# One decoder layer in a single launch: the order of helper work around its engines' queues is rewritten in four places

## The chip, the cores and the metric

The kernel runs on one core of one Trainium2 chip, in one launch. The metric is the device time of that launch in microseconds (us), the median over several runs. The core's engines are TensorE (PE: matmuls and transposes, with PEld for its weight loads), VectorE (DVE), ScalarE (ACT), GpSimd (POOL) and SyncE (SP, which here only issues DMAs). Each works through its own list of instructions in order and meets the others at semaphores.

## The reference, cut to what matters

Input x is (2, 1024, 256) float32: 2 batches, 1024 tokens, 256 features; the kernel cuts the 2048 tokens into 4 blocks of 512 and each block into 4 tiles of 128.

```
# 1 gated linear attention, 16 heads, DK = 8, DV = 16
q, k, v = x@Wq, x@Wk, x@Wv;  gk = log_sigmoid(x@Wgk1@Wgk2 + b)/16
h_t = h_{t-1}*exp(gk_t) + k_t v_t ;   o_t = (q_t * 8**-.5) h_t
x = layernorm(x + (rmsnorm(o)*gnw*silu(x@Wg)) @ Wo)
# 2 cross attention: each token attends to 64 of 64 context rows, given by an index
#   list with repeats; the kernel counts how often each row is named
x = layernorm(x + softmax(q k[idx]^T) v[idx] @ W_out)
# 3 causal self attention, 16 heads, then 8 experts, top 2, gelu
h = ln1(x); a = attention(h)@Wo + bo + x
h2 = ln2(a); w = softmax over the two best of (h2@Wr + br)
x = layernorm(sum_e w_e * (gelu(h2@w1_e + b1_e)@w2_e + b2_e) + a)
```

## The kernel before, in words

The program is four `nc.Block`s, one behind another. In each block every engine has its own list, written by hand.

**First block, `front` (0 to about 210 us).** The recurrence is a hardware scan along the 1024 tokens. There are NJ = 32 steps `jj` (2 batches by 16 value columns). In a step VectorE does three 128x1024 operations: `product(jj)` (L521, the k-v product out of PSUM), `state(jj)` (L526, the scan) and `output(jj)` (L531, times q). Its loop runs `state(jj)`, then `product(jj+1)`, then `output(jj)`. Other VectorE work is slipped into this loop at a named step, either behind `state(jj)` or behind `output(jj)`: `parts_lo(n)` (L514, low half of a split of the values, needed by PE and waiting for ScalarE's `parts_hi(n)`, L680), `x_lo` (L505, waits for ScalarE's `x_hi`, L650), `log_sigmoid(1)` (L511, waits for ScalarE's logarithm, L666), `out_means(m)` (L836, waits for ScalarE's `out_square(m)`, L832), and `out_gated(m)` (L845 to L849, waits for ScalarE's `out_root(m)`, L840). All `out_` helpers finish token block m; blocks 0 and 1 share one buffer, so `out_square(1)` comes behind `out_copy(0)` (L857), and that behind PE's transposes of what `out_gated(0)` wrote.

ScalarE has a list by the same `jj`. Into its gaps go 65 operations `signs` (L695, one 128x1024 comparison each, for counting the context indices). The list `taken` says how many of them are done by each step. In the steps with jj a multiple of 4, ScalarE copies the head sums (`sums_out`, L685), does one sign, then copies what PE has turned meanwhile (`tokens`, L688).

**Third block, `attend` (about 356 to 628 us).** Eight groups of four heads, `g` = 0 to 7. PE computes scores in units for the row maxima (VectorE, L2074), turns the maxima into rows (`turn`), computes scores again for the exponentials (ScalarE, L2012) and multiplies by values (`pv`, L1859). `warm(n, bank)` issues n matmuls of 128x512 whose result nobody reads (L1866). They stand at the start, ahead of `turn(0)` (7), behind the first unit of group 1 (3), behind the work of each of the first three steps `c` of group 0 (2 each), and at the end (2 and 2).

The last group is written out apart: its quads of exponentials (`last_exps(k)`, L2033; `quad_scores(k)` and `quad_sums(k)` on PE, k = 0 to 9) are interleaved with the routing work of token block 0. That work is one chain: `turn_sums`, `divide`, `turn_rows`, copies, `project` (L122), `residual` and statistics, `deviation` (ScalarE's square root, L2252), `normed` (L2308), `turn_normed` (L114), the two copies `rows_hi` and `normed_copy`, `logits` (L2237), the best two, and the weights. Scores of a quad reuse PSUM banks: bank b waits for the exponential of bank b-4. So `quad_scores(k)` waits for the first exponentials of quad k-1.

**Fourth block, `moe` (628.7 to 1384.6 us).** PE runs through s = 0 to 255 (32 pairs of expert and token block, 8 slices each): `first_layer` for s (6 matmuls, L2451), then `second_layer` for s-3 (6 matmuls, L2464). ScalarE applies gelu (L2533), VectorE splits the result (L2598, L2600). `first_layer(s)` waits for gelu(s-2). Weights come in quarters (n, q): SP loads a quarter to one of two raw buffers (L2193), ScalarE makes the high part (`weights_hi`, L2198), VectorE the low part (`weights_lo`, L2203). A load waits for the low part of the quarter two places earlier. `second_layer` of expert 0 waits for the low part of its quarter 3. The bias table is transposed by PE first (L2491) and copied by ScalarE (L2535).

Of the kernel before, what the change touches and what calls it, by code (L numbers as in the profile page):

```python
# [17 lines left out]
ACT = mybir.ActivationFunctionType  # L18
# [19 lines left out]
E = 8  # L38
# [23 lines left out]
class Kernel:  # L62
# [99 lines left out]
    def front(self, c):  # L162
# [58 lines left out]
        taken = list(itertools.accumulate((0, 1, 2, 3, 3, 5, 2, 1, 1, 1, 1, 2, 2, 3, 2, 3, 1, 2, 2, 2, 2, 2, 2, 2, 3, 3, 2, 2, 2, 2, 2, 1)))  # L221
# [3 lines left out]
        with nc.Block() as block:  # L225
# [268 lines left out]
            def _(e):  # L494
# [69 lines left out]
                for jj in range(NJ):  # L564
                    state(jj)
                    if jj == 2:
                        parts_lo(1)
                    elif jj == 6:
                        x_lo(3, 4)
                    elif jj == 11:  # L570
                        log_sigmoid(1)
                    elif jj == 12:
                        parts_lo(2)
                    elif jj == 18:
                        self.out_means(e, 0)
                    elif jj == 19:
                        parts_lo(3)
                    elif jj == 23:
# [6 lines left out]
                    if jj == 3:  # L585
                        x_lo(2, 4)
                    elif jj == 19:
                        self.out_gated(e, 0)
                        self.out_means(e, 1)
                    elif jj == 21:  # L590
# [42 lines left out]
            def _(e):  # L633
# [92 lines left out]
                for jj in range(NJ):  # L726
                    if jj % 4 == 0 and jj:
# [3 lines left out]

                        signs(range(taken[jj - 1], taken[jj - 1] + 1))
# [62 lines left out]
                    signs(range(taken[jj - 1] + (jj % 4 == 0) if jj else 0, taken[jj]))  # L795
# [758 lines left out]
    def attend(self, c):  # L1554
# [81 lines left out]
        with nc.Block() as block:  # L1636
# [93 lines left out]
            def _(e):  # L1730
# [172 lines left out]
                warm(7, 7)  # L1903
# [4 lines left out]
                warm(3, 7)  # L1908
                for g in range(NG - 1):
                    for c in range(NS):  # L1910
# [19 lines left out]

                        if g == 0 and c < PV_AT[0][0]:
                            warm(2, 7)
# [49 lines left out]
            def _(e):  # L1982
# [60 lines left out]
                last_exps(5)  # L2043
                last_exps(6)
                self.deviation(e, 0)
# [174 lines left out]
    def project(self, e, m, rb, ts=range(TB)):  # L2220
        if 0 in ts:
            e.wait_ge(self.VR.sem, self.VR.at("onT0", m))
            e.wait_ge(self.AR.sem, self.AR.at("onT1", m))
        last = self.token_major(e, self.onT, self.Wo, rb, ts)
        if TB - 1 in ts:
            last.then_inc(self.SR.sem, 1)
# [120 lines left out]
    def moe(self, c):  # L2347
# [54 lines left out]
        with nc.Block() as block:  # L2402
# [32 lines left out]
            def _(e):  # L2435
# [55 lines left out]
                e.transpose(PS[:, RB[0], 0:E * (NF + KD)], self.eb[:, :], self.ident[0:E * (NF + KD), 0:E * (NF + KD)]).then_inc(SM.sem, 1)  # L2491
# [31 lines left out]
            def _(e):  # L2523
# [11 lines left out]
                e.activation(bias[:, :], PS[:, RB[0], 0:E * (NF + KD)], ACT.Copy).then_inc(A.sem, 1)  # L2535
                e.wait_ge(A.sem, A.at("b1"))
                for s in range(NI * NF):
# [48 lines left out]
            def _(e):  # L2586
# [46 lines left out]
                def last_normed(k):  # L2633
# [6 lines left out]
                    last.then_inc(VL.sem, 1)  # L2640
                for s in range(NI * NF):
# [7 lines left out]
                    if s < 2:  # L2649
                        self.weights_lo(e, 0, 2 + s)  # L2650
                    elif 4 <= s < 8:
                        self.weights_lo(e, 1, s - 4)
# [97 lines left out]
```

## Time and the profile before

| | |
|---|---|
| median of 3 runs | 1386.23 us (1383.28 to 1386.34) |
| the profiled execution: its time | 1386.34 us |
| its span, first to last instruction | 1384.6 us |
| around the span | 1.74 us |
| mean granted TensorE clock | 0.982 |
| busy: PE / PEld / DVE / ACT / POOL | 93% / 69% / 71% / 47% / 10% |

Busy shares are averages over four blocks with different limits, so the profile is read block by block. The rows of a timeline give the start and the length of an instruction (or of several alike, then with xcount), and in brackets how long its engine had stood idle and who released it. An engine issues its next operation a little before the last one's recorded end, so the distance of two starts is used for pitch.

### The profile page before, as it was taken

Reading aid. Unit: us, or ns where it says so; the run is one execution under the profiler, and the core shown is the slowest. Engines: PE = TensorE matmul, PEld = TensorE weight load, DVE = VectorE, ACT = ScalarE, POOL = GpSimd, SP = SyncE. Lnnn points to the kernel's source line nnn. Section 1 sums busy time; section 2 is a strip of 40 time slices with the busy share of each in tenths; the row PEclk is TensorE's granted clock in tenths of the full one; section 3 lists DMA queues with packets and bytes.
Section 4 is the critical chain, followed back from the end, with each engine's and each line's share of the span. In section 5 each row is a group of like instructions: output and inputs, shape, how many; then the busy total and the mean of one; then the engine's idle time right before and its main releaser. Section 6 shows DMA issues by size and latency. Waiting matters only on the chain.

```text
span 1384.6 us, 18774 instructions
## 1 busy us (share of the span) xinstructions
PE 1291.7 (93%) x7481; PEld 953.4 (69%) x7481; DVE 977.6 (71%) x1409; ACT 647.3 (47%) x946; POOL 138.7 (10%) x217
## 2 busy tenths in 40 slices
PE   8786768999899999999999999999999999999997
PEld 6363437656655554556888888888888888888886
DVE  7998986798688888866666656655656555556566
ACT  5778564436457877784333333322322323232233
POOL 5000002000513434211000000000000000000000
PEclk9999989999999999999999999999999999999999
DMA  4000001001632221213000012110201102010001
GB/s 138 1 1 0 0 1 35 0 1 69 194 102 58 58 61 57 66 31 108 9 8 17 0 39 69 47 38 16 69 16 43 42 16 69 16 39 16 0 16 46
DMA packets 38599, 55.76 MB, mean 40 GB/s; under 512 B 8976, under 2 KB 23744, under 8 KB 38512
## 3 DMA queue, kind: packets, MB, share of 16 engines
q1 hardware_dynamic: 33328, 43.67, 10.3%
q0 software_dynamic: 3648, 10.09, 2.6%
q8 instruction: 59, 0.97, 0.3%
q10 hardware_dynamic: 1536, 0.81, 0.2%
q14 instruction: 28, 0.23, 0.1%
HBM read 43.73 MB, written 10.55 MB: 39 GB/s over the span
## 4 chain that ended last, share of the span: by engine, by line
PE 51%; DVE 2%; ACT 1%; issue 0%; ACTq 0%; DVEq 0%
PE PS L2451 24%; PE PS L2464 24%; PE PS L122 1%; PE PS L114 0%; PE PS L2477 0%; PE PS L2212 0%; PE PS L2237 0%; DVE OT_all L2607 0%; DVE r_st L2291 0%; DVE r_on L2308 0%; DVE r_on L2288 0%; PE PS L2489 0%; DVE X L2300 0%; DVE x_mid L2598 0%; ACT X L2570 0%
## 5 line engine op out<-in xcount | busy, mean ns | idle before, releaser
L2533 ACT ACTIVATE x_g<-PS,x_bias 128x512 f32<-128x512 f32 x256 | 175.9, 687 | 494.0 <-PE PS L2451 493.6
L2451 PE MATMUL PS<-x_h,x_w 128*128 128x512 f32 x1536 | 399.8, 396 | 0.6 <-ACT x_g L2533 0.6
L2464 PE MATMUL PS<-x_mid,x_w 128*128 128x512 f32 x1488 | 383.9, 393 | 1.2 <-DVE x_w L2203 1.2
L2451 PEld LDWEIGHTS PS<-x_h,x_w 128*128 128x128 f32 x1536 | 286.1, 188 | 66.1 <-ACT x_g L2533 1.5
L2464 PEld LDWEIGHTS PS<-x_mid,x_w 128*128 128x128 f32 x1488 | 279.4, 188 | 65.6 <-DVE x_w L2203 1.7
L2598 DVE CAST x_mid<-x_g 128x512 fp32r<-128x512 f32 x256 | 109.3, 427 | 271.6 <-ACT x_g L2533 271.5
L2074 DVE TENSOR_REDUCE a_M<-PS 128x2 f32<-128x1024 f32 (+1 forms) x144 | 170.6, 1222 | 24.9 <-PE PS L1782 19.3
L2600 DVE TENSOR_TENSOR x_mid<-x_g,x_mid 128x512 fp32r<-128x512 f32 x256 | 177.2, 692 | 8.8
L2012 ACT ACTIVATE f_parts<-PS 128x512 f32<-128x512 f32 x224 | 121.2, 600 | 34.4 <-PE PS L1836 27.9
L1859 PE MATMUL PS<-f_parts,aV 128*32 128x256 f32 (+1 forms) x960 | 74.2, 390 | 0.2 <-POOL f_parts L1673 0.2
L526 DVE TENSOR_TENSOR_SCAN qh<-decay,qh 128x1024 f32<-128x1024 f32 x32 | 73.0, 2283 | 0.0
L695 ACT ACTIVATE c_hot<-c_idxT,c_cid 128x1024 bf16<-128x1024 bf16 x65 | 70.7, 1137 | 3.5 <-PE PS L337 2.2
L2431 POOL DMA_DIRECT2D x_wb<-route_w x31 | 16.8, 541 | 476.3 <-DVE OT_all L2607 453.4
L1836 PE MATMUL PS<-aQ,aK 64*128 64x512 f32 x192 | 50.0, 489 | 0.0
L307 PE MATMUL PS<-vparts,g_sel 128*128 128x512 f32 x128 | 41.1, 448 | 8.6 <-DVE qh L521 7.6
L1836 PEld LDWEIGHTS PS<-aQ,aK 64*128 64x128 f32 x192 | 19.6, 183 | 39.7 <-ACT f_parts L2012 28.3
L2607 DVE SCALAR_TENSOR_TENSOR OT_all<-PS,x_bias,x_wb 128x512 f32<-128x512 f32 x62 | 46.2, 745 | 0.0
L1778 PE MATMUL PS<-aK,aQ 64*128 64x512 f32 (+3 forms) x256 | 36.0, 336 | 9.8 <-DVE a_M L2074 7.1
L1673 POOL TENSOR_SCALAR_AFFINE_SELECT f_parts<-f_parts 128x512 f32<-128x512 f32 x45 | 28.6, 635 | 164.6 <-ACT f_parts L2012 145.1
L2203 DVE TENSOR_TENSOR x_w<-x_raw,x_w 128x1024 fp32r<-128x1024 f32 x32 | 39.2, 1228 | 2.0 <-ACT x_w L2198 2.0
L521 DVE TENSOR_TENSOR qh<-PS,KT 128x1024 f32<-128x1024 f32 x32 | 38.6, 1207 | 2.7 <-PE PS L314 1.3
L531 DVE TENSOR_TENSOR qh<-qh,QT 128x1024 f32<-128x1024 f32 x32 | 38.9, 1216 | 0.0
(371 smaller groups left out, 1582.8 us busy)
## 6 DMA issues: line engine op xcount, KB each, us to landing
x_raw<-L_ffn_e_w SPq DMA_DIRECT2D x32, 512.0 KB, 3.7
qk_parts<-f_parts SPq DMA_DIRECT2D x16, 512.0 KB, 3.9
x_wb<-route_w POOLq DMA_DIRECT2D x31, 256.0 KB, 3.3
aK<-qk_parts SPq DMA_DIRECT2D x96, 64.0 KB, 2.6
aQ<-qk_parts SPq DMA_DIRECT2D x96, 64.0 KB, 2.5
X<-x SPq DMA_DIRECT2D x4, 512.0 KB, 7.5
out<-X SPq DMA_DIRECT2D x3, 512.0 KB, 2.9
O<-itok_BxSx SPq DMA_DIRECT2D x2, 256.0 KB, 7.8
```

Source lines behind the costliest of these rows:

```text
L526: e.tensor_tensor_scan(qh[:, jj % RQ, :], decay[:, batch(jj // HD)], qh[:, jj % RQ, :], 0.0, ALU.mult, ALU.add).then_inc(s_h, 1)
L695: e.activation(hot[:, n % RS, :], self.idxT[:, :], ACT.Sign, bias=self.cid[:, c:c + 1], scale=2.0).then_inc(s_sg, 1)
L1836: last = e.matmul(bank, K[q][R, s, tile(TB * h if kind == "k0" else kind)], Q[q][R, s, q0:q0 + BLK], start=True, stop=True)
L1859: last = e.matmul(PS[32 * j:32 * j + 32, 7, dst:dst + w], Vs[m % 2][:, kt, j, :], x, start=k in (0, 3) and half == 0, stop=k in (2, NQD - ...
L2012: e.activation(buf[k][:, j, :], PS[:, 4 + b % 3, :], ACT.Exp).then_inc(A.sem, 1)
L2074: e.tensor_reduce(dst, src, AX.X, ALU.max, negate=True).then_inc(VC.sem, 1)
L2451: last = e.matmul(PS[:, f % 2, :], w1[n % 2][u][:, kt, f * P:(f + 1) * P], self.rows(v, k)[:, kt, :], start=m == 0 and kt == 0, stop=m == ...
L2464: last = e.matmul(PS[:, 2 + 2 * (it % 2) + d, :], w2[n % 2][v][:, f, d * P:(d + 1) * P], mid[u][:, f % RM, :], start=f == 0 and m == 0, st ...
L2533: e.activation(g[s % RG][:, :], PS[:, f % 2, :], ACT.Gelu, bias=b1[:, n, f:f + 1]).then_inc(A.sem, 1)
L2598: e.tensor_copy(mid[0][:, f % RM, :], g[s % RG][:, :]).then_inc(V.sem, 1)
L2600: e.tensor_tensor(mid[1][:, f % RM, :], g[s % RG][:, :], mid[0][:, f % RM, :].bitcast(F32), ALU.subtract).then_inc(V.sem, 1)
L2607: e.scalar_tensor_tensor(out=(y if n else sumT[k])[:, d, :], in0=PS[:, 2 + 2 * (it % 2) + d, :], scalar=b2[:, n, d:d + 1], in1=wb[:, it % ...
```

## The change

1. **`front`, VectorE.** `parts_lo`, `x_lo(3)`, `log_sigmoid(1)` and `out_means(0)` move from behind `state(jj)` to behind `output(jj-1)`. `out_gated(0)` moves from behind `output(19)` to behind `output(18)`, and `out_gated(1)` from 21 to 20. `out_means(1)` stays behind `output(19)`.
2. **`front`, ScalarE.** The sign between `sums_out` and `tokens` goes, and the list `taken` is new. The total stays 65.
3. **`attend`.** 12 of the filling matmuls go: 3 of the 7 ahead of `turn(0)`, the 3 behind the first unit, 6 in group 0. In the last group `project` is one piece ahead of `quad_scores(5)`, scores come ahead of sums, `turn_normed` comes ahead of `quad_sums(6)` and `logits` ahead of `quad_sums(7)`; the two pairs of filling matmuls stand ahead of `project` and of `turn_normed` and no longer at the end. ScalarE's `deviation(0)` comes ahead of `last_exps(6)`.
4. **`moe`.** The bias transposes go to PSUM bank 0, and PE waits for ScalarE's copy of them before its first matmul. `weights_hi` and `weights_lo` of expert 0's quarters 2 and 3 run ahead of the loop (before: in s = 0 and 1). Expert 1's four quarters are made high in s = 1 to 4 and low in s = 2 to 5 (before: both in s = 4 to 7).

```
-taken = accumulate((0, 1, 2, 3, 3, 5, 2, 1, 1, 1, 1, 2, 2, 3, 2, 3, 1, 2, 2, 2, 2, 2, 2, 2, 3, 3, 2, 2, 2, 2, 2, 1))
+taken = accumulate((0, 1, 1, 2, 2, 3, 3, 2, 2, 2, 3, 2, 2, 3, 2, 3, *[2] * (HD - 1), 1))
 # front, VectorE
                     state(jj)
-                    if jj == 2: parts_lo(1)
-                    elif jj == 6: x_lo(3, 4)
-                    elif jj == 11: log_sigmoid(1)
-                    elif jj == 12: parts_lo(2)
-                    elif jj == 18: self.out_means(e, 0)
-                    elif jj == 19: parts_lo(3)
 ...
                     output(jj)
+                    if jj == 1: parts_lo(1)
-                    if jj == 3:
+                    elif jj == 3:
                         x_lo(2, 4)
+                    elif jj == 5: x_lo(3, 4)
+                    elif jj == 10: log_sigmoid(1)
+                    elif jj == 11: parts_lo(2)
+                    elif jj == 17: self.out_means(e, 0)
+                    elif jj == 18:
+                        parts_lo(3)
+                        self.out_gated(e, 0)
                     elif jj == 19:
-                        self.out_gated(e, 0)
                         self.out_means(e, 1)
-                    elif jj == 21:
+                    elif jj == 20:
                         self.out_gated(e, 1)
 # front, ScalarE
                         sums_out(jj // 4 - 1)
-                        signs(range(taken[jj - 1], taken[jj - 1] + 1))
                         tokens(jj // 4 - 1)
 ...
-                    signs(range(taken[jj - 1] + (jj % 4 == 0) if jj else 0, taken[jj]))
+                    signs(range(taken[jj - 1] if jj else 0, taken[jj]))
 # attend, PE
-                warm(7, 7)
+                warm(4, 7)
 ...
-                warm(3, 7)
 ...
-                        if g == 0 and c < PV_AT[0][0]:
-                            warm(2, 7)
 ...
                 quad_sums(NG - 1, 2)
-                self.project(e, 0, FREE, range(2))
-                quad_scores(5)
-                self.project(e, 0, FREE, range(2, TB))
-                for k in range(6, 8):
-                    quad_sums(NG - 1, k - 3)
+                warm(2, SPARE)
+                self.project(e, 0, FREE)
+                for k in range(5, 8):
                     quad_scores(k)
-                quad_sums(NG - 1, 5)
+                    quad_sums(NG - 1, k - 2)
+                warm(2, SPARE)
+                self.turn_normed(e, 0, FREE)
                 quad_sums(NG - 1, 6)
-                self.turn_normed(e, 0, FREE)
                 quad_scores(8)
+                self.logits(e, 0, FREE)
                 quad_sums(NG - 1, 7)
-                self.logits(e, 0, FREE)
                 quad_scores(9)
                 quad_sums(NG - 1, 8)
-                warm(2, SPARE)
                 quad_sums(NG - 1, 9)
-                warm(2, SPARE)
 # attend, ScalarE
                 last_exps(5)
+                self.deviation(e, 0)
                 last_exps(6)
-                self.deviation(e, 0)
 # moe, PE
-                e.transpose(PS[:, RB[0], 0:E * (NF + KD)], self.eb[:, :], ...).then_inc(SM.sem, 1)
+                e.transpose(PS[:, 0, 0:E * (NF + KD)], self.eb[:, :], ...).then_inc(SM.sem, 1)
+                e.wait_ge(A.sem, A.at("b1"))
 # moe, ScalarE (VectorE alike: weights_lo, with s in (2, 3, 4, 5) and s - 2)
+                for q in range(2, 4):
+                    self.weights_hi(e, 0, q)
 ...
-                    if s < 2:
-                        self.weights_hi(e, 0, 2 + s)
-                    elif 4 <= s < 8:
-                        self.weights_hi(e, 1, s - 4)
+                    if s in (1, 2, 3, 4):
+                        self.weights_hi(e, 1, s - 1)
```

## Rows read from the trace of the kernel before

**Rows 1.** Windows, first and last block: length; PE, PEld, DVE, ACT, POOL busy; clock.
```profile
0.00:210.00 210.00, 160.12 (x873) 101.85 (x874) 189.91 (x166) 142.14 (x152) 18.39 (x52) 0.91 0.08 23
...
628.70:1384.60 755.90, 743.49 (x3361) 607.58 (x3361) 452.81 (x812) 240.03 (x332) 18.86 (x35) 1.00 0.11 34
```

**Rows 2.** Timeline of VectorE, first block.
```profile
36.01 1.20 DVE L514 TENSOR_TENSOR vparts<-PS,vparts 128x1024 fp32r<-128x1024 f32 x1
...
44.49 1.23 DVE L505 TENSOR_TENSOR XTp<-PS,XTp 128x1024 fp32r<-128x1024 f32 x1 [0.57 <-ACT XTp L650]
...
57.64 1.22 DVE L505 TENSOR_TENSOR XTp<-PS,XTp 128x1024 fp32r<-128x1024 f32 x1 [0.83 <-ACT XTp L650]
...
65.49 2.28 DVE L526 TENSOR_TENSOR_SCAN qh<-decay,qh 128x1024 f32<-128x1024 f32 x1
...
81.04 1.20 DVE L511 SCALAR_TENSOR_TENSOR z<-z,decay 128x1024 f32<-128x1024 f32 x1
...
86.99 1.23 DVE L514 TENSOR_TENSOR vparts<-PS,vparts 128x1024 fp32r<-128x1024 f32 x1 [0.28 <-ACT vparts L680]
...
115.46 1.22 DVE L836 TENSOR_REDUCE go_ms<-z 128x64 f32<-128x1024 f32 x1 [0.53 <-ACT z L832]
...
131.71 1.22 DVE L836 TENSOR_REDUCE go_ms<-z 128x64 f32<-128x1024 f32 x1 [4.12 <-ACT z L832]
```

**Rows 3.** Timeline of ScalarE, first block.
```profile
34.68 1.03 ACT L680 ACTIVATE vparts<-PS 128x1024 fp32r<-128x1024 f32 x1 [3.70 <-PE PS L292]
...
79.79 1.06 ACT L666 ACTIVATE decay<-decay 128x1024 f32<-128x1024 f32 x1
...
85.93 1.02 ACT L680 ACTIVATE vparts<-PS 128x1024 fp32r<-128x1024 f32 x1 [2.10 <-PE PS L292]
...
114.36 1.06 ACT L832 ACTIVATE z<-O 128x1024 f32<-128x1024 f32 x1
```

**Rows 4.** Part 5 of the page, the sign operations.
```profile
L695 ACT ACTIVATE c_hot<-c_idxT,c_cid 128x1024 bf16<-128x1024 bf16 x65 | 70.7, 1137 | 3.5 <-PE PS L337 2.2
```

**Rows 5.** Windows of PE: length, busy (count), granted clock, DMA share, GB/s.
```profile
110.00:112.00 2.00, 0.00 (x0) 1.00 0.00 0
112.00:114.00 2.00, 1.86 (x17) 1.00 0.00 0
152.00:154.00 2.00, 0.00 (x0) 1.00 0.00 0
...
156.00:158.00 2.00, 2.00 (x10) 0.50 0.00 0
```

**Rows 6.** Timeline of PE, start of the third block.
```profile
398.29 0.73 PE L1866 MATMUL PS<-a_idr 128*128 128x512 f32 x2
```

**Rows 7.** Timeline of VectorE, start of the third block.
```profile
401.25 5.86 DVE L2074 TENSOR_REDUCE a_M<-PS 128x8 f32<-128x1024 f32 x5 [1.10 <-PE PS L1782]
```

**Rows 8.** Timeline of ScalarE, last group of the third block.
```profile
609.79 2.06 ACT L2033 ACTIVATE V<-PS 128x512 f32<-128x512 f32 x4 [0.63 <-PE PS L1836]
613.37 2.06 ACT L2033 ACTIVATE V<-PS 128x512 f32<-128x512 f32 x4 [1.52 <-PE PS L1836]
615.45 1.28 ACT L2252 ACT_TABLE_LOAD   x1
616.75 0.30 ACT L2252 ACTIVATE r_sd<-r_mv,eps 128x4 f32<-128x4 f32 x1
```

**Rows 9.** Timeline of PE, last group of the third block.
```profile
609.86 1.99 PE L122 MATMUL PS<-r_Wo,r_onT 128*128 128x256 f32 x8
...
618.73 1.09 PE L114 MATMUL PS<-ident,r_on 128*128 128x128 f32 x8 [0.88 <-DVE r_on L2308]
```

**Rows 10.** Timeline of PE, start of the fourth block.
```profile
637.49 1.66 PE L2464 MATMUL PS<-x_mid,x_w 128*128 128x512 f32 x6 [1.22 <-DVE x_w L2203]
```

**Rows 11.** Timeline of SP's queue, fourth block.
```profile
647.26 0.38 SPq L2193 DMA_DIRECT2D x_raw<-L_ffn_e_w  x1
```

**Rows 12.** Timeline of ScalarE, fourth block.
```profile
652.07 1.06 ACT L2198 ACTIVATE x_w<-x_raw 128x1024 fp32r<-128x1024 f32 x1 [0.74 <-DMA x_raw<-L_ffn_e_w]
```

More of the change, by code:

```diff
@@ L219, in front @@
         vt_banks = lambda n: 4 if n else 0
-        taken = list(itertools.accumulate((0, 1, 2, 3, 3, 5, 2, 1, 1, 1, 1, 2, 2, 3, 2, 3, 1, 2, 2, 2, 2, 2, 2, 2, 3, 3, 2, 2, 2, 2, 2, 1)))
+        taken = list(itertools.accumulate((0, 1, 1, 2, 2, 3, 3, 2, 2, 2, 3, 2, 2, 3, 2, 3, *[2] * (HD - 1), 1)))
         assert taken[-1] == NCTX
@@ L565, in _ @@
                     state(jj)
[L566 to L578, printed above, removed]
+                    if jj == 23:
                         self.out_rstd(e, 0)
@@ L584, in _ @@
                     output(jj)
-                    if jj == 3:
+                    if jj == 1:
+                        parts_lo(1)
+                    elif jj == 3:
                         x_lo(2, 4)
+                    elif jj == 5:
+                        x_lo(3, 4)
+                    elif jj == 10:
+                        log_sigmoid(1)
+                    elif jj == 11:
+                        parts_lo(2)
+                    elif jj == 17:
+                        self.out_means(e, 0)
+                    elif jj == 18:
+                        parts_lo(3)
+                        self.out_gated(e, 0)
                     elif jj == 19:
-                        self.out_gated(e, 0)
                         self.out_means(e, 1)
-                    elif jj == 21:
+                    elif jj == 20:
                         self.out_gated(e, 1)
@@ L2218, in turn_rows, with project @@
         self.transposes(e, self.on, 0, rb).then_inc(self.SR.sem, 1)
[L2220 to L2226, printed above, removed]
+    def project(self, e, m, rb):
+        e.wait_ge(self.VR.sem, self.VR.at("onT0", m))
+        e.wait_ge(self.AR.sem, self.AR.at("onT1", m))
+        self.token_major(e, self.onT, self.Wo, rb).then_inc(self.SR.sem, 1)
     def turn_normed(self, e, m, rb):
@@ L2490, in sums_turned @@
                     last.then_inc(SF.sem, 1)
-                e.transpose(PS[:, RB[0], 0:E * (NF + KD)], self.eb[:, :], self.ident[0:E * (NF + KD), 0:E * (NF + KD)]).then_inc(SM.sem, 1)
+                e.transpose(PS[:, 0, 0:E * (NF + KD)], self.eb[:, :], self.ident[0:E * (NF + KD), 0:E * (NF + KD)]).then_inc(SM.sem, 1)
+                e.wait_ge(A.sem, A.at("b1"))
                 for s in range(NI * NF):
@@ L2534, in _ @@
                 e.wait_ge(SM.sem, SM.at("b1"))
-                e.activation(bias[:, :], PS[:, RB[0], 0:E * (NF + KD)], ACT.Copy).then_inc(A.sem, 1)
+                e.activation(bias[:, :], PS[:, 0, 0:E * (NF + KD)], ACT.Copy).then_inc(A.sem, 1)
+                for q in range(2, 4):
+                    self.weights_hi(e, 0, q)
                 e.wait_ge(A.sem, A.at("b1"))
@@ L2640, in last_normed @@
                     last.then_inc(VL.sem, 1)
+                for q in range(2, 4):
+                    self.weights_lo(e, 0, q)
                 for s in range(NI * NF):
@@ L2648, in _ @@
                         summed(it - 1)
[L2649 to L2652, printed above, removed]
+                    if s in (2, 3, 4, 5):
+                        self.weights_lo(e, 1, s - 2)
                     if m + 1 < NB:
```

## Prediction, made before the change was run

> **What bounds the kernel now.** I read the windows by block first. In the last block TensorE is busy 743.5 of 755.9 us at full clock, in the first VectorE 189.9 of 210.0 us [rows 1]. The chain that ended last holds, for the last block, TensorE's two matmul lines nearly alone. So the kernel is four blocks in a row: the first goes by VectorE, the last by TensorE, and what a helper costs is read from the waits of these two. Then I read the timelines around each edit: VectorE and ScalarE in the first block, TensorE and ScalarE in the last head group, all of them where the experts start. The reader is to see in the bracket of a row who was late, and by how much. The rows that follow are used as terms.
>
> No edit changes an operation on data, except that 12 filling matmuls go. All else is order, so each term is a difference of waits.
>
> **First block, VectorE.** A helper moved from behind `state(jj)` to behind `output(jj-1)` comes one scan sooner: 2.28 us as recorded, 2.2 as pitch [rows 2]. It waits for its supplier on ScalarE that much longer, less what VectorE is already late, plus what the supplier is late.
> - `parts_lo(1)`: its supplier ends at 34.68 + 1.03 = 35.71 [rows 3]. The slot moves from 36.01 [rows 2] to 33.8. Wait 1.9, before 0. VectorE is 1.9 late, and 1.4 after `x_lo(2)`, whose wait of 0.57 [rows 2] is filled.
> - `x_lo(3)`: 0.83 before [rows 2]; 0.83 + 2.2 - 1.4 = 1.6, less about 0.5 since the sign ahead of `tokens` is gone and ScalarE gets there sooner: 1.1. VectorE is 1.6 late.
> - `log_sigmoid(1)`: the logarithm ends at 79.79 + 1.06 = 80.85 [rows 3], the slot moves from 81.04 to 78.8, that is 2.0 short. The new list asks for 4 signs in steps 7 and 8 where 2 stood. A sign is 1.14 [rows 4]; about half of the 2.3 goes into waits of ScalarE, so the supplier is 1.0 late. 2.0 - 1.6 + 1.0 = 1.4. VectorE is 3.0 late.
> - `parts_lo(2)`: steps 9 and 10 hold 5 signs where 2 stood, 3.4 more; ScalarE's wait of 2.10 ahead of this supplier [rows 3] takes 2.1 of them. Supplier late: 1.0 + 3.4 - 2.1 = 2.3. Wait 0.28 + 2.2 - 3.0 + 2.3 = 1.8, before 0.28 [rows 2]. VectorE is 4.5 late.
> - `out_means(0)`: from there to `out_square(0)` (114.36 [rows 3]) the lists hold 14 signs against 13, and in steps 12 and 16 the sign that used to run while TensorE turned the sums now runs after: 2.3 + 1.1 + 0.9 = 4.3 late. Wait 0.53 + 2.2 - 4.5 + 4.3 = 2.5, before 0.53 [rows 2].
> - `out_means(1)`: before, it stood right behind `out_gated(0)` and waited 4.12 [rows 2] for TensorE, a copy and the square. Now step 19 (scan and two products, 4.5) lies between: wait 0. `out_gated` itself waits 0.2 at most.
>
> New waits 1.9 + 1.1 + 1.4 + 1.8 + 2.5 = 8.7, old ones 0.57 + 0.83 + 0.28 + 0.53 + 4.12 = 6.3. **First block +2.4.** Bounds: suppliers on time after the first item, 1.9 - 6.3 = -4.4; suppliers one sign later each than reckoned, +5.
>
> **Third block, start.** VectorE waited 1.10 for the second unit of group 1 [rows 7]; two pairs of filling matmuls, 0.66 of pitch a pair, 0.73 as recorded [rows 6], stood ahead of that unit, but the exponentials that its neighbours wait for gain only some 0.3. The seven ahead of `turn(0)` only cover a wait for VectorE. Behind 401.25 VectorE runs five maxima without a gap [rows 7]. I take -0.5; bounds -1.1 (the whole wait) and +1.7 (clock, below).
>
> **Third block, last group.** Ahead of `quad_scores(5)` come the second half of the projection (1.99 recorded, 1.9 pitch [rows 9]) and a filling pair (0.66). So `last_exps(5)` starts at 609.79 [rows 8] + 2.5 = 612.3 and ends at 614.4. The projection's own end doesn't move: the pair replaces four score matmuls of the same length. Then ScalarE has the root: a table load of 1.28 [rows 8], the root, and a second load, some 2.9 together. They stood behind `last_exps(6)`; now they stand ahead, so `last_exps(6)` starts at 617.25, not 613.37 [rows 8]. Queued behind it on TensorE are `quad_scores(7)` (needs those banks), sums 5, a filling pair and only then `turn_normed`. Scores end at 617.25 + 2.06 + 0.2 = 619.5, sums 1.0, pair 0.66: `turn_normed` at 621.2, not 618.73 [rows 9], though its input is there by 617.3. The order behind is a chain of the same pieces (scores 8, exponentials, scores 9, POOL's mask, last sums, their copy on ScalarE), and the pair that stood at the very end was mostly under waits. **+2.6.** Bounds: -1.4, if only the earlier root counts, and +4.6 with a lower clock.
>
> The price of a switch of tables decides here. A load is recorded at 1.28, 615.45 to 616.73, and the root starts at 616.75 [rows 8]; I use that. The Trainium skill (ScalarE: Activation LUTs, "What ACT_TABLE_LOAD costs") adds a drain of 1.38 us to each load, 2.66 in all; by it the term would be 2.8 us more. By that rule the root could not start 0.02 us behind its load, as it does here.
>
> **Fourth block, start.** TensorE reached `second_layer(0)` 637.49 - 628.7 = 8.8 us into the block, the last 1.22 waiting for the low half of quarter 3 [rows 10]. Now both quarters are ready before the first gelu is split. The wait for the bias copy (an estimate: 0.45) and two high halves ahead of gelu(0) delay the third slice by 0.6, most of which its later neighbour takes up; `second_layer(0)` comes at 7.4, a gain of 1.4. Against it: ScalarE now stands at expert 1's quarters from s = 1 on and its gelus queue behind. A load takes 4.8 from issue (647.26 [rows 11]) to ScalarE's start (652.07, after waiting for the DMA [rows 12]). Quarter 3 of expert 1 is asked for at about 12.7 into the block, lands at 17.5, and gelu(5) comes at 19.0 to 19.7, where TensorE is ready at 18.8: 0.9 lost. **-0.5.** Bounds -1.4 and +1.5 (both late loads met in full).
>
> **The clock.** TensorE's granted clock stayed at 1.00 over an empty window at 110 to 112 us, but after another at 152 to 154 it stood at 0.50 (1.2 in place of 2.4 GHz) [rows 5]. Two new gaps are like these: about 615.4 to 617.6 and then four matmuls in two us; and the joint of the last two blocks, where the last filling pair is gone. I take one fall, in one of them. At half clock sums 5, the pair and `turn_normed` (2.7 us at full) take 2.7 more, or the first four slices twice their length with ScalarE covering half; about 1.5 reaches the end.
>
> **Sum**: 2.4 - 0.5 + 2.6 - 0.5 + 1.5 = +5.5. The profiled execution took 1386.34 us (span 1384.6 and 1.7 around it), 0.1 over the median. 1386.3 + 5.5 = 1391.8.
>
> **Rivals.**
> - *The clock holds.* All else as above: +4.0, 1390.3. For it: [rows 5], first two. Chance 0.22. It lies within 0.3% (4.2 us), which is what a measurement of this kernel can tell from no change.
> - *The first block gains* (not slower). ScalarE keeps up: with the sign ahead of `tokens` gone, everything that TensorE hangs on the sums comes a sign sooner, and the 4.12 counts. It decides at `parts_lo(2)`: if its supplier ends by 86.95, as now [rows 3], the later waits vanish. Block -4.4, the rest +1.6 without a fall: 1383.5. Against it: three more signs there than ScalarE has idle time for. Chance 0.22, with the tail's term also smaller in some of it, so that 0.08 is beyond 0.3%.
> - *Loads hold the gelus* (slower). If expert 1's loads land late, each blocked gelu stops TensorE: fourth block +1.5 in place of -0.5: 1393.8. For it: 4.8 of latency against 2.8 per slice. Chance 0.16.
> - *A load blocks longer than recorded* (slower). Would each of the two loads of the last group hold ScalarE for twice its 1.28, now that its exponentials queue behind them, the group would lose 2.6 more: 1394.4. The load in [rows 8] shows no such time: chance 0.03. The Trainium skill's page named above states a rule of this kind.
>
> The forecast itself has 0.37. **Chances**: slower by over 0.3% 0.37 + 0.16 + 0.03 = 0.56 less 0.02 for the forecast's own low end; within 0.3% 0.22 + 0.14 + 0.02; faster 0.08. **Range** 1384.5 to 1395.0: it leaves out the faster end of the second rival and the tail beyond the last; the forecast's own is 1389.5 to 1394.
>
> **What would show it.** Right: VectorE waits of 1 to 3 us at `parts_lo(1)`, `x_lo(3)`, `log_sigmoid(1)`, `parts_lo(2)` and `out_means(0)`, none at `out_means(1)`, the first block about 2.4 longer; ScalarE's root between exponentials 5 and 6, `turn_normed` about 2.5 later, the fourth block starting at 633 to 635; `second_layer(0)` 7.4 after its start. Wrong: signs that TensorE waits for less than I think, or a tail in which the scores of quad 7 don't wait for ScalarE.

## The result: 10.8 us slower, where 5.5 were forecast

| | before | after |
|---|---|---|
| median | 1385.38 us (1383.28 to 1386.34, 4 runs) | 1396.65 us (1394.47 to 1398.4, 4 runs) |
| ratio | | 1.0078, 95% interval 1.0058 to 1.0097: +8.0 to +13.4 us, +10.8 in the middle |
| profiled execution | 1386.34 us, span 1384.6, clock 0.982 | 1390.58 us, span 1388.9, clock 0.979 |

The profiled execution of the changed kernel is the fastest of its thirteen. The others ran 1391.5 to 1399.3 us, with a mean granted clock between 0.979 and 0.970. So its trace shows where the waits are, but only part of the loss: of 10.8 us it holds 4.3 in the span. The kernel before has one more run here than ahead of the prediction, which moved its median from 1386.23 to 1385.38.

Windows of the changed kernel, first and last block, columns as in [rows 1]:

```profile
0.00:210.00 210.00, 157.89 (x869) 100.81 (x870) 189.53 (x164) 141.63 (x152) 18.60 (x52) 0.91 0.08 23
...
632.84:1388.90 756.06, 744.80 (x3361) 608.50 (x3361) 452.61 (x812) 239.95 (x332) 18.82 (x35) 0.99 0.11 34
```

The last block keeps its length (756.1 for 755.9 us) and starts 4.1 us later. Timeline of VectorE in the first block, the operations of [rows 2] in the changed kernel:

```profile
35.89 1.22 DVE L514 TENSOR_TENSOR vparts<-PS,vparts 128x1024 fp32r<-128x1024 f32 x1 [1.85 <-ACT vparts L680]
...
56.72 1.23 DVE L505 TENSOR_TENSOR XTp<-PS,XTp 128x1024 fp32r<-128x1024 f32 x1 [0.68 <-ACT XTp L650]
...
80.20 1.23 DVE L511 SCALAR_TENSOR_TENSOR z<-z,decay 128x1024 f32<-128x1024 f32 x1
...
87.36 1.22 DVE L514 TENSOR_TENSOR vparts<-PS,vparts 128x1024 fp32r<-128x1024 f32 x1 [1.48 <-ACT vparts L680]
...
117.42 1.22 DVE L834 TENSOR_REDUCE go_ms<-z 128x64 f32<-128x1024 f32 x1 [2.15 <-ACT z L830]
...
131.66 1.21 DVE L834 TENSOR_REDUCE go_ms<-z 128x64 f32<-128x1024 f32 x1
...
139.29 0.55 DVE L843 RECIPROCAL go_rs<-go_rs 128x64 f32<-128x64 f32 x1 [1.97 <-ACT go_rs L838]
```

Four waits are where and as long as reckoned: 1.85 (1.9 forecast), 1.48 (1.8), 2.15 (2.5) and none where 4.12 stood. `x_lo(3)` waits 0.68 (1.1). `log_sigmoid(1)` doesn't wait (1.4 forecast), and `out_gated(1)` waits 1.97 (0.2). The block ends only 0.9 later than in the trace of before (first copy into `aug` at 212.4 against 211.6), but how little such a pair of traces says is shown below.

Timeline of ScalarE and then of TensorE in the last head group, against [rows 8, 9]:

```profile
611.93 2.06 ACT L2024 ACTIVATE V<-PS 128x512 f32<-128x512 f32 x4 [2.81 <-PE PS L1834]
614.01 1.28 ACT L2240 ACT_TABLE_LOAD   x1
615.31 0.30 ACT L2240 ACTIVATE r_sd<-r_mv,eps 128x4 f32<-128x4 f32 x1
615.62 1.28 ACT L2024 ACT_TABLE_LOAD   x1
616.92 2.07 ACT L2024 ACTIVATE V<-PS 128x512 f32<-128x512 f32 x4
```

```profile
617.57 1.96 PE L1834 MATMUL PS<-aQ,aK 64*128 64x512 f32 x4 [2.02 <-ACT V L2024]
...
621.99 1.67 PE L114 MATMUL PS<-ident,r_on 128*128 128x128 f32 x8
```

`last_exps(6)` starts at 616.92 (617.25 forecast). The scores of quad 7 wait 2.02 for it, and `turn_normed`, its input ready at 617.3, is queued behind them until 621.99 (621.2 forecast). The lengths show more: eight transposes take 1.67 where they took 1.09 [rows 9]. Windows of TensorE (length, busy, granted clock, DMA share, GB/s) show why, and two more such places:

```profile
394.00:396.00 2.00, 1.04 (x4) 0.65 0.00 0
402.00:404.00 2.00, 2.00 (x19) 0.50 0.00 0
...
618.00:620.00 2.00, 2.00 (x16) 0.97 0.00 0
620.00:622.00 2.00, 2.00 (x15) 0.50 0.00 0
622.00:624.00 2.00, 2.00 (x17) 0.68 0.00 0
634.00:636.00 2.00, 2.00 (x6) 0.50 0.00 0
```

The clock is at half (1.2 GHz) from some 395 to 405 us, where the fillers were removed, from 620 to 623, behind the 2 us without work, and from 633.5 to 637, just behind the joint to the fourth block. I had counted one fall. Between 364 us and the last ten us this execution has three, and that of before none; it lacks the other's fall at the joint of the second and third block, 356 to 363.

### The profile page after: what moved, and what is told of

The parts are those of the page before. It is cut to its first block, busy times and chain, and to the rows that moved or that the text cites. A ratio compares the mean times of both kernels' runs of the same rounds, so it can differ in the third digit from the quotient of the medians.

```text
span 1388.9 us, 18750 instructions
## 1 busy us (share of the span) xinstructions
PE 1291.1 (93%) x7469; PEld 954.1 (69%) x7469; DVE 978.2 (70%) x1409; ACT 646.8 (47%) x946; POOL 138.9 (10%) x217
## 4 chain that ended last, share of the span: by engine, by line
PE 50%; DVE 3%; ACT 1%; issue 0%; DMA 0%; ACTq 0%; DVEq 0%
PE PS L2439 24%; PE PS L2452 23%; PE PS L122 1%; PE PS L114 0%; PE PS L2465 0%; DMA x_raw<-L_ffn_e_w 0%; PE PS L2225 0%; DVE OT_all L2596 0%; DVE r_st L2279 0%; DVE r_on L2296 0%; DVE x_mid L2589 0%; DVE x_mid L2587 0%; DVE r_on L2276 0%; PE PS L2477 0%; PE PS L2203 0%
## 5 line engine op out<-in xcount | busy, mean ns | idle before, releaser
L307 PEld LDWEIGHTS PS<-vparts,g_sel 128*128 128x128 f32 x128 | 23.6, 202 | 25.0 <-DVE qh L521 15.6
```

The source lines that it names most:

```text
L307: last = e.matmul(PS[:, 2 * (jj % 2) + half, :], self.sel[:, j, :], vparts[:, u, n % 2, half * BLK:(half + 1) * BLK], start=u == 0, stop=u ...
```

## The experiments

Each ran in alternation with the kernel before. "+us" is the ratio less one, times the median of before (1384.7 to 1386.5). "Clock" is the mean over all executions; that of before was 0.9816 to 0.9823.

| kernel | +us (95% interval) | clock |
|---|---|---|
| the whole change | +10.8 (8.0 to 13.4) | 0.9741 |
| front_alone | +3.9 (2.2 to 5.5) | 0.9799 |
| warms_alone | +0.7 (-1.4 to 2.8) | 0.9791 |
| tail_alone | +7.1 (4.3 to 9.7) | 0.9783 |
| experts_alone | +1.5 (-0.3 to 3.3) | 0.9802 |
| tail_dev_back | +2.6 (0.8 to 4.3) | 0.9813 |
| dev_alone | +5.0 (3.3 to 6.7) | 0.9805 |
| tail_fill_back | +3.6 (1.7 to 5.5) | 0.9798 |
| dve_alone | +1.8 (0.0 to 3.5) | 0.9807 |
| signs_alone | +4.2 (2.4 to 6.0) | 0.9794 |
| signs_counts | +2.1 (0.7 to 3.5) | 0.9793 |
| signs_place | +1.0 (-0.3 to 2.2) | 0.9805 |
| experts_fill | +0.6 (-1.4 to 2.5) | 0.9811 |
| after_fill_back | +6.8 (4.4 to 9.2) | 0.9777 |
| after_fill_dev_back | +4.2 (2.2 to 6.1) | 0.9790 |
| after_three_back | -0.8 (-2.8 to 1.2) | 0.9814 |
| after_dev_signs_back | +1.8 (-1.0 to 4.6) | 0.9782 |
| joint_fill | -0.6 (-1.9 to 0.7) | 0.9814 |
| three_joint | -0.8 (-3.3 to 1.5) | 0.9823 |

### The four parts, each alone

The change's diff cut in four by place: first block (`taken`, the signs, VectorE's helpers), the fillers at the start of the third block, its last head group, the start of the fourth block. In the expectations theory Q lays a loss to waits in the engines' queues, theory C to TensorE's clock.

> Of the change only the first block's part: VectorE's helpers and the sign operations in their new places, the rest as before. Theory Q (the loss of each part is the wait that its queue gets): the waits seen in the trace of the changed kernel sum to some 7 us on VectorE against 6.3 before, the block ended 0.85 us later: +0.5 to +1.5 us, granted clock as before (0.982). Theory C (the loss is TensorE's clock, which falls more often): this part removes no TensorE work, so it is the one part in which C expects little too, 0 to +2 us; but if its time moves together with a lower mean granted clock, C has its hand here as well. The forecast had +2.4 us for it, and a rival -4.

> Of the change only the filler matmuls at the joint of the second and third block: 4 for 7 ahead of the turn, none behind the first units and none between the first scores. Theory Q: the path there is VectorE's and ScalarE's, and fewer matmuls in front of the scores give 0 to -1 us. Theory C: the fillers held the clock; without them TensorE runs at 1.2 GHz from some 394 to 405 us, in every execution, and the kernel is 1.5 to 4 us slower, with a mean granted clock lower by 0.004 or more.

> Of the change only the last head group: the projection in one piece, scores ahead of sums, the deviation ahead of the exponentials of group 6, the closing fillers moved forward. Theory Q: the root between two loads of ScalarE's tables stands ahead of an exponential that scores(7) waits for: +2.5 to +4 us by the end of the block and no more, at the clock of before. Theory C: the same +2.5 to +4 us, and on top of it the clock that falls at the end of the group and over the joint to the fourth block, where the fillers no longer stand: +4 to +7 us, with a lower mean clock than before in most executions.

> Of the change only the start of the fourth block: bias through bank 0, the first layer waiting for it, the copies of the weights' halves earlier. Theory Q: the second layer starts 0.3 us earlier after the block's start, the copies that wait for their loads cost nothing on TensorE: 0 to -0.5 us. Theory C: TensorE waits idle at the block's start for the bias, and its clock falls there: +0.5 to +2 us with a lower mean clock.

They sum to +13.2, within what 10.8 (8.0 to 13.4) allows: the loss is in the parts and not in their company. The last group is the largest, +7.1 where 2.6 stood, and the first block came out above its expectation. In the trace of tail_alone the stretch from `turn_rows` to `turn_normed` is 17.73 us (600.47 to 618.20) against 13.78 before (from 604.95 to the 618.73 of [rows 9]), and the fourth block's first matmul to `second_layer(0)` 9.54 against 8.78. Windows of TensorE in tail_alone:

```profile
612.00:614.00 2.00, 0.87 (x2) 0.74 0.00 0
616.00:618.00 2.00, 2.00 (x14) 0.50 0.00 0
630.00:632.00 2.00, 2.00 (x7) 0.51 0.00 0
```

warms_alone kept its promise about the clock and not about the time. Windows of TensorE:

```profile
392.00:394.00 2.00, 1.61 (x10) 0.50 0.03 8
396.00:398.00 2.00, 2.00 (x20) 0.50 0.00 0
400.00:402.00 2.00, 2.00 (x18) 0.50 0.00 0
```

All three traced kernels without these fillers have a clock of 0.80 over 385 to 410 us; all others, 17 traces, have 1.00. But its median is +0.7 and not +1.5 or more: what the clock costs there is about paid back by matmuls that no longer stand ahead of the units.

### The last group taken apart

tail_dev_back and dev_alone differ from tail_alone and from before in this alone:

```diff
                 last_exps(5)
-                self.deviation(e, 0)
                 last_exps(6)
+                self.deviation(e, 0)
```
(dev_alone: the reverse). tail_fill_back:
```diff
-                warm(2, SPARE)
                 self.project(e, 0, FREE)
...
-                warm(2, SPARE)
                 self.turn_normed(e, 0, FREE)
...
                 quad_sums(NG - 1, 8)
+                warm(2, SPARE)
                 quad_sums(NG - 1, 9)
+                warm(2, SPARE)
```

> The last head group's new order as in tail_alone (which measured +7.1 us), but ScalarE's deviation back behind the exponentials of group 6. Theory A (the deviation ahead of them is the loss: its two table loads and its root, 2.9 us, stand between scores(6) and the exponentials that free scores(7)'s banks, and turn_normed is queued behind scores(7)): exps(6) then follows exps(5) directly, the root comes about 0.7 us later after the first turn than in the kernel before, turn_normed 14.4 to 14.6 us after it (before 13.8, tail_alone 17.7); the kernel is +0.5 to +2.5 us against before. Theory B (the order on TensorE and the fillers' place are the loss, whatever ScalarE does): +5 us or more stay.

> The kernel before with one thing changed: the deviation ahead of the exponentials of group 6. ScalarE is idle there for 1.5 us before them, so of 2.9 us some 1.4 come to lie on them. Theory A: exps(6) 1.4 us later, scores(7) and sums(6) with it, turn_normed waits for sums(6) on the queue: +0.5 to +2 us. Theory B: what the deviation costs the exponentials it gives back to the chain of the routing, 0 +/- 0.7 us.

> As tail_alone, but the two pairs of filling matmuls stand behind the last sums as in the kernel before, not ahead of the projection and of turn_normed. Theory A: ahead of the projection they held exps(5) 0.6 us back, at the end they are hidden: +5.5 to +7 us stay of +7.1. Theory C (the clock at the joint): without them at the end TensorE falls to 1.2 GHz at the fourth block's start (tail_alone, 630 to 633 us), and with them there the clock holds at that place: the second layer starts within 8.9 us of the block's start, and +3.5 to +5.5 us stay.

Theory A holds. With the deviation back, 4.5 of 7.1 us are gone (the +2.6 that stay are at the top of its +0.5 to +2.5), and `turn_normed` comes 14.34 us behind `turn_rows` (607.26 to 621.60). Timeline of ScalarE in tail_dev_back: the exponentials of quads 5 and 6 run as one stretch of eight, and the root follows.

```profile
614.28 4.03 ACT L2030 ACTIVATE V<-PS 128x512 f32<-128x512 f32 x8 [2.81 <-PE PS L1836]
618.32 1.28 ACT L2246 ACT_TABLE_LOAD   x1
619.62 0.30 ACT L2246 ACTIVATE r_sd<-r_mv,eps 128x4 f32<-128x4 f32 x1
```

dev_alone was to cost 0.5 to 2 and cost 5.0: one line moved by one place. I had overlooked a wait. Timelines of ScalarE and of TensorE in dev_alone:

```profile
610.78 1.28 ACT L2252 ACT_TABLE_LOAD   x1
614.08 0.30 ACT L2252 ACTIVATE r_sd<-r_mv,eps 128x4 f32<-128x4 f32 x1 [2.02 <-DVE r_mv L2298]
614.40 1.28 ACT L2033 ACT_TABLE_LOAD   x1
615.69 2.06 ACT L2033 ACTIVATE V<-PS 128x512 f32<-128x512 f32 x4
```

```profile
616.34 2.26 PE L1836 MATMUL PS<-aQ,aK 64*128 64x512 f32 x4 [2.92 <-ACT V L2033]
...
622.11 1.75 PE L114 MATMUL PS<-ident,r_on 128*128 128x128 f32 x8
```

The root's table is loaded, and then ScalarE stands 2.02 us for VectorE's statistics, with exponentials queued behind whose scores ended at 612.4. TensorE stands 2.92 us, and its clock goes to half: 0.50 from 618 to 622 us. In the changed kernel `last_exps(5)` comes 7.0 us behind `turn_rows` and not 4.8 as here, so the root doesn't wait and TensorE's gap is 2.02; the rest is the same.

tail_fill_back stays at +3.6: 3.5 us less than tail_alone, though the intervals overlap. Its fourth block starts at full clock (1.00 over 628 to 638 us, tail_alone 0.83) and reaches `second_layer(0)` in 8.79 us, as before. Both statements of theory C came in, the time at the low edge of its +3.5 to +5.5; that of A didn't. But the trace doesn't show that the fillers held the clock. A fall stands just ahead of them, and over the whole end of the block the clock is what it is in tail_alone. Window of TensorE in tail_fill_back, then 580 to 640 us in tail_alone, tail_fill_back, dev_alone and tail_dev_back:

```profile
624.00:627.00 3.00, 3.00 (x28) 0.50 0.02 5
580.00:640.00 60.00, 53.09 (x422) 0.89 0.10 30
580.00:640.00 60.00, 54.26 (x424) 0.89 0.10 31
580.00:640.00 60.00, 54.02 (x449) 0.91 0.07 21
580.00:640.00 60.00, 54.66 (x489) 0.97 0.06 19
```

What the time at half clock follows here is the deviation. The five traces with it ahead of the exponentials of quad 6 (the first three of these kernels, the changed kernel and after_fill_back) have 7 to 14 us at half clock between 580 and 640 us, 11.6 in the mean. The fifteen others have 0 to 7, 2.9 in the mean, wherever the fillers stand. What the 3.5 us between tail_alone and tail_fill_back are stays open; that run moves both pairs and doesn't part them.

### The first block taken apart

dve_alone has only the moved helpers, signs_alone only what ScalarE's sign operations change, and that again in two:
```diff
-        taken = list(itertools.accumulate((0, 1, 2, 3, 3, 5, 2, 1, 1, 1, 1, 2, 2, 3, 2, 3, 1, 2, 2, 2, 2, 2, 2, 2, 3, 3, 2, 2, 2, 2, 2, 1)))
+        taken = list(itertools.accumulate((0, 1, 1, 2, 2, 3, 3, 2, 2, 2, 3, 2, 2, 3, 2, 3, *[2] * (HD - 1), 1)))
```
in signs_counts, and in signs_place
```diff
                         sums_out(jj // 4 - 1)
-                        signs(range(taken[jj - 1], taken[jj - 1] + 1))
                         tokens(jj // 4 - 1)
...
-                    signs(range(taken[jj - 1] + (jj % 4 == 0) if jj else 0, taken[jj]))
+                    signs(range(taken[jj - 1] if jj else 0, taken[jj]))
```

> Of the first block's part (which measured +3.9 us) only the places of VectorE's helpers; ScalarE's sign operations as before. Theory Q (a helper that comes an iteration before its input is ready stalls VectorE, and the chain of states behind it): all of the part's loss is here, +2.5 to +5 us. Theory S (the signs' new counts shift ScalarE, which then gives vparts, z and states later): 0 to +1.5 us here, and the rest with the signs.

> Of the first block's part only the sign operations' new counts on ScalarE (the part measured +3.9 us, VectorE's helpers alone +1.8 us). If the two add up: +1 to +3 us. If the signs cost nothing and the helpers only collide with them: 0 +/- 0.7 us.

> Of the signs' change (+4.2 us) only the new counts per step; one sign still stands ahead of tokens in every fourth step. If the counts are the cause (three or four signs in a row ahead of copies that TensorE waits for): +3 to +5 us. If the place is: 0 to +1 us.

> Only the sign ahead of tokens taken away, its work put behind the step's other copies, the counts as before. ScalarE then waits idle for TensorE's sums and turns in eight steps and does the sign after, when TensorE waits for copies: 1.1 us each, partly hidden. If this is the cause: +3 to +5 us, with ScalarE's waits ahead of L688 up by about 1 us each. If the counts are: 0 to +1 us.

It was mainly the signs: +4.2 (2.4 to 6.0) alone, above what was expected even if the two added up, against +1.8 (0.0 to 3.5) for the helpers. These two intervals overlap; the traces below and after_three_back point the same way. Timeline of VectorE in signs_alone, where every helper is in its old place, and in dve_alone:

```profile
81.05 1.22 DVE L511 SCALAR_TENSOR_TENSOR z<-z,decay 128x1024 f32<-128x1024 f32 x1 [1.56 <-ACT decay L666]
88.19 1.23 DVE L514 TENSOR_TENSOR vparts<-PS,vparts 128x1024 fp32r<-128x1024 f32 x1 [1.45 <-ACT vparts L680]
118.29 1.22 DVE L834 TENSOR_REDUCE go_ms<-z 128x64 f32<-128x1024 f32 x1 [2.17 <-ACT z L830]
134.46 1.22 DVE L834 TENSOR_REDUCE go_ms<-z 128x64 f32<-128x1024 f32 x1 [4.12 <-ACT z L830]
```

```profile
35.80 1.23 DVE L514 TENSOR_TENSOR vparts<-PS,vparts 128x1024 fp32r<-128x1024 f32 x1 [1.85 <-ACT vparts L680]
58.87 1.22 DVE L505 TENSOR_TENSOR XTp<-PS,XTp 128x1024 fp32r<-128x1024 f32 x1 [2.94 <-ACT XTp L650]
88.26 1.23 DVE L514 TENSOR_TENSOR vparts<-PS,vparts 128x1024 fp32r<-128x1024 f32 x1 [0.34 <-ACT vparts L680]
116.71 1.22 DVE L836 TENSOR_REDUCE go_ms<-z 128x64 f32<-128x1024 f32 x1 [0.55 <-ACT z L832]
137.79 0.55 DVE L845 RECIPROCAL go_rs<-go_rs 128x64 f32<-128x64 f32 x1 [0.70 <-ACT go_rs L840]
```

Three waits are new in the first, against 0, 0.28 and 0.53 in [rows 2]: together 4.4 us. The 4.12 stays. ScalarE's timeline of signs_alone shows a run of two and one of three signs, 2.17 and 3.22 us, ahead of the supplier of `parts_lo(2)`, which it reaches at 87.14 without the wait of 2.10 that it had [rows 3]. In dve_alone the helpers wait 1.85 and 2.94 for their early places, and the 4.12 is gone: about even. Counts and place make +2.1 and +1.0. Neither comes to the +3 to +5 of a single cause; the counts are told from nothing, the place isn't, and the two aren't told from each other.

The traces allow a second reading. The first block ends (first copy into `aug`) at:

| helpers, signs | traces | mean | lowest and highest |
|---|---|---|---|
| old, old | 9 | 211.4 us | 208.9, 214.3 |
| new, old | 4 | 210.0 | 209.2, 210.9 |
| old, new | 1 | 213.3 | |
| new, new | 4 | 214.5 | 212.4, 215.5 |

(signs_counts ends at 211.9, signs_place at 213.8.) So by the means the part is +3.1, the signs +4.5 with the new helpers around them, the helpers nothing or a small gain. But nine traces of one and the same first block differ by 5.4 us: the 0.9 us that the first pair of traces showed can't be told from chance.

The clock goes with these ends. Up to the copy, six of the nine old ones have 34 to 38 us at half clock and end at 208.9 to 211.6; the other three have 44 and end at 213.4 to 214.3. Of the new, new ones the changed kernel has 38 and ends at 212.4; the other three have 44 and end at 215.0 to 215.5. At like clock the part is thus +1.2 to +2.4, about the size of the forecast, and the rest goes with more time at half clock. The new, old ones have 34 to 38 and end where the old ones with as much do.

### The causes taken away one after the other

after_fill_back is the changed kernel with all fillers in their old places; after_fill_dev_back has the deviation back as well; after_three_back also the old signs. after_dev_signs_back is the last of these with the change's fillers.

> The whole change, but every filling matmul of the kernel before in its old place (7 ahead of the turn, 3 behind the first units, 6 in group 0, two pairs behind the last sums; none ahead of the projection and of turn_normed). Theory C (most of the change's +10.8 us is the clock: over the executions of one kernel a us more at 1.2 GHz costs about 0.4 us, and the changed kernel has some 74 us of them against 49 to 51 before): the mean granted clock goes back from 0.974 to 0.977 or more and +4 to +8 us stay. Theory Q (queues): +9.5 to +11 us stay, since the fillers lie beside other work.

> The same, and the deviation back behind the exponentials of group 6. From dev_alone (+5.0 us) and tail_dev_back (4.5 us less than tail_alone) it should be 3.5 to 5 us faster than after_fill_back, with turn_normed 14 to 15 us behind the first turn: +1 to +4 us against before. If deviation and fillers pay for one and the same fall of the clock, less: 1 to 2.5 us.

> The whole change less signs, deviation and the moved fillers: left are VectorE's helpers, the order of scores and sums with the projection in one piece, and the fourth block's start. From the single runs: +1.8 for the helpers, +1.5 for the fourth block, 0 to +2 for the order, if they add up +3 to +4.5 us; if signs and helpers share one loss, or the parts' losses are mostly falls of the clock in other places, 0 to +2 us. In no case more than after_fill_dev_back's +4.2.

> The whole change less deviation and signs; only its fillers (10 of 16 gone at the start of the third block, the last two pairs moved forward) differ from after_three_back, which measured -0.8 us. If the fillers are a cause of their own: +2 to +4 us, with TensorE at 1.2 GHz from some 392 to 404 us and at the fourth block's start. If they only cost where a stall had already put the clock at risk: -0.5 to +1 us.

+10.8, +6.8, +4.2, -0.8: fillers 4.0, deviation 2.6, signs 5.0, and nothing is left. VectorE's helpers, the projection in one piece with the new order of scores and sums, and the start of the fourth block cost together what can't be told from zero, below my expectation of +3 to +4.5 and near the 0 to +2 of its other branch. The deviation gave 2.6 here and not 3.5 to 5, but the intervals of the two runs allow both. Taken as differences of independent runs, the three steps are known to about 3.6, 3.0 and 2.8 us either way, an estimate: the deviation's share isn't told from zero by this pair, but it is by dev_alone.

The fillers are less sure. Alone as a suspect (12 of the 16 are gone at the start of the third block, not the 10 that the expectation names) they make +1.8 (-1.0 to 4.6), 2.6 more than without and, by their intervals, not told from it. Windows of TensorE in that kernel have the fall at the start of the third block again:

```profile
396.00:398.00 2.00, 1.25 (x4) 0.60 0.04 8
402.00:404.00 2.00, 2.00 (x18) 0.50 0.00 0
```

That they lower the clock is shown (0.9782 against 0.9814). That this costs 4 us wherever they go, and not mainly beside the stall of the last group, isn't.

### Tries at something faster

experts_fill is experts_alone with two fillers ahead of the wait for the bias; joint_fill the kernel before with 12 for 8 fillers at the end of the second block; three_joint is after_three_back with those 12.
```diff
+                for _ in range(2):
+                    e.matmul(PS[:, RB[0], :].rearrange("p (c n) -> p c n", n=P), self.identr[:, :], self.identr[:, :].unsqueeze(1).broadcast_to((P, 4, P)), start=True, stop=True)
                 e.wait_ge(A.sem, A.at("b1"))
...
                 e.wait_ge(V3.sem, V3.at("y", m))
-                for _ in range(8):
+                for _ in range(12):
```

> The kernel before with the change's fourth block (which measured +1.5 us at a mean clock of 0.980 against 0.982, though its second layer began 0.5 us earlier after the block's start), and two filling matmuls on TensorE ahead of its wait for the bias. Theory C: the loss was the clock that falls at the block's start, the fillers hold it, 0 to -1.5 us, a clock of 0.982 or more. Against it: the fillers' 0.5 us lie partly on the path and the clock falls in spite of them: +1 to +2 us.

> The kernel before with 12 for 8 filling matmuls at the end of the second block. The clock falls there (some 356 to 366 us) in about half of the traces, after an idle time of TensorE of 2.7 us. If the fillers hold it: 0 to -1.5 us and a mean clock above 0.982. If they only end later than the block's other engines: 0 to +1 us.

> after_three_back (-0.8 us) with joint_fill's 12 for 8 filling matmuls at the end of the second block (-0.6 us alone). If they add up: -1 to -2 us. If both were chance within the spread of the runs: 0 +/- 0.7 us.

+0.6, -0.6 and -0.8, none told from the kernel before. In both traces with the twelve fillers the clock is 1.00 over 356 to 366 us, where 9 of the 18 others fall; two traces don't show that the fillers hold it, and no gain is seen in the time. In experts_fill the clock holds at the start of the block and `second_layer(0)` comes 7.35 us into it (628.42 to 635.77) against 8.78 before; of these 1.4 us the median shows nothing, and where they go stays open. No version beats the kernel before.

## Why the prediction was right or wrong

**The direction and the places were right, the size was short by half.** The forecast was 1391.8 in a range of 1384.5 to 1395.0; the median was 1396.65, outside the range.

- **"The clock. I take one fall ... about 1.5 reaches the end": this is the step that failed.** The thirteen executions have a mean clock of 0.974 where before has 0.982. Twice the span times what is missing from 1 is the time at half clock: 72 us against 49 to 51. My one fall held 5.4 us at half clock (2.7 us of work at twice its length); the runs have 22 more. Within one kernel the executions tell its price: over the first eight variants and their runs of before, a us more at half clock goes with 0.39 us more time (0.32 over the changed kernel's own thirteen). 22 us times 0.39 are 8.6, an estimate, since a wait of TensorE may lengthen the time and lower the clock at once, and this counts both. Taken at its face it leaves 2.2 of 10.8 for all else; the deviation and the signs cost more than that, so by this reckoning part of their loss is the clock's. What I had left out is that the new waits elsewhere go with a lower clock too, the first block's among them: signs_alone, with another order of sign operations only, has 57 us at half clock where its runs of before have 51. The Trainium skill (TensorE: Matmul & The Clock Gate, "HAM oscillation — how this bites in real kernels") counts half of the throttled time as penalty. The runs here give 0.39 in place of 0.5; a reason may be that the first block goes by VectorE [rows 1], but no run tests it.
- **The last group, +2.6**: the mechanism was right to 0.8 us in each row. Alone it measured +7.1 (4.3 to 9.7), beyond its bound of 4.6. Its trace holds 4.0 by `turn_normed` where 2.5 was reckoned, then 1.1 up to the fourth block and 0.8 in it. Half clock stands in all three stretches or next to them (613 to 620 and 630 to 633.5 us). "The pair that stood at the very end was mostly under waits" priced its absence at nothing. With both pairs back the run is 3.5 us faster, the intervals overlapping, and whether the clock is the reason isn't shown: tail_fill_back falls as long as tail_alone, a little earlier, and experts_alone and after_three_back, with the pair in its place but the change's start of the fourth block, fall behind the joint all the same (632 to 635.5 and 630 to 633.6).
- **The first block, +2.4**: +3.1 by the means of the traces, +3.9 (2.2 to 5.5) by the runs. Right in size, the more so at like clock (+1.2 to +2.4), and in five of seven waits; the text laid it to the moved helpers, with the signs as a correction. It is the other way round.
- **The start of the third block, -0.5**: +0.7 (-1.4 to 2.8). The bound of +1.7 was the clock's, and the fall came each time.
- **The fourth block, -0.5**: +1.5 (-0.3 to 3.3) alone, nothing in after_three_back. In the trace of experts_alone `second_layer(0)` comes 8.24 us into the block, with a clock of 0.83 over 628 to 638 us; 7.4 was forecast, and experts_fill, where the clock holds, has 7.35. With the clock held the step was right to 0.1 us, and still the median of experts_fill shows no gain.
- **The rivals.** The clock didn't hold. The first block didn't gain: at `parts_lo(2)`, where I had put the decision, the supplier ended at 87.3 and not by 86.95. Late loads did hold ScalarE, 4.76 us in the changed kernel, yet TensorE stood 0.35 at the most in the stretch behind. The table loads stay at 1.28 us with exponentials queued behind them: in the changed kernel the first ends at 615.29 and the root starts at 615.31. The longer price of the Trainium skill (ScalarE: Activation LUTs, "What ACT_TABLE_LOAD costs") isn't seen here either.

Timelines of ScalarE and of TensorE in the changed kernel, for the loads:

```profile
647.37 1.06 ACT L2189 ACTIVATE x_w<-x_raw 128x1024 fp32r<-128x1024 f32 x1 [4.76 <-DMA x_raw<-L_ffn_e_w]
```

```profile
656.05 1.09 PE L114 MATMUL PS<-ident,r_on 128*128 128x128 f32 x8 [0.35 <-DVE r_on L2262]
```

## What to carry to other kernels

A stall of TensorE can be priced twice, once as the wait and once as the matmuls at half clock behind it (dev_alone: 2.92 us of wait, then 0.50 from 618 to 622), though not every stall is followed by a fall [rows 5]. Sum over all places where the change thins out its work, not over the one that looks worst, and count the time at half clock in several executions of each version. A wait that an in-order engine meets early (the root ahead of the exponentials) holds what is queued behind it, so look up when its input is ready, not only what it costs. And a pair of traces can't settle a difference of one or two us in a stretch whose length varies by five: give such a part its own runs.

## What the runs showed of the hardware that was not expected

- The first block, with the same code, ended between 208.9 and 214.3 us in nine traces, later where it had 44 us at half clock and not 34 to 38, and executions of the kernel before spread from 1381.3 to 1389.3 us with a mean clock of 0.985 to 0.980. The time at half clock differs from execution to execution of one program.
- Twelve filling matmuls at the start of the third block, 0.33 us each by the pitch of a pair (0.66), decide whether 10 us there run at 2.4 or 1.2 GHz (17 traces with them, 3 without), and the median hardly moves (+0.7, -1.4 to 2.8).
- ScalarE loads the table of an operation ahead of that operation's wait: in dev_alone the load ended at 612.06 and the root still waited 2.02 for its input. So the first load was hidden under the wait; the second, 1.28 us, stood behind the root (614.40) and wasn't.
